# Local transformer: the norm of the MLP's rows on GpSimd behind its softmax product, its turning products and copies one step later

## The chip, the cores and the metric

One core of a Trainium2 chip runs the whole kernel, one launch. The metric is the device time of that core in microseconds, the median of several runs; lower is better.

## The reference

The kernel computes a chain of four transformer-like layers on x of shape (4, 512, 128). The change is in the third, a local transformer of six layers, 16 heads of 64, windows of 32 rows:

```
for i in range(DEPTH):                       # DEPTH = 6
    x = attn_layer(shift_tokens(x), Wqkv[i], q_scale[i], k_scale[i], Wo[i]) + x
    x = ffn_layer(shift_tokens(x), ln_g[i], ln_b[i], W1[i], b1[i], W2[i], b2[i]) + x

def ffn_layer(x, g, bln, W1, b1, W2, b2):
    mu = x.mean(-1, keepdims=True)
    var = ((x - mu) ** 2).mean(-1, keepdims=True)
    xn = (x - mu) / jnp.sqrt(var + 1e-05) * g + bln
    hg = xn @ W1 + b1
    a, gate = jnp.split(hg, 2, -1)
    return a * jax.nn.gelu(gate, approximate=False) @ W2 + b2
```

`attn_layer` makes q, k and v, scales q and k to unit length, turns them by rotary tables, takes a softmax over the own and the previous window, and projects back. All of it is float32.

## The kernel before

The four batches go through the transformer in pairs, so its six layers are twelve half-layers (`hl`, 0 to 11). The attention of a half-layer is eight steps (`w`, 0 to 7; `g` = 8 hl + w counts all 96 of them), one for every half of a unit of 128 rows by two batches. The work of several steps is in flight at once: while step g takes its softmax, the rotary products of step g + 3 and the transposes of step g + 2 are made. The order of each engine's instructions is written out by hand, in one loop over g for each engine (`tensor`, `vector`, `scalar`, `gpsimd`); engines wait for each other by counting semaphores (`s.at(name, n)`).

The MLP of a half-layer needs all rows of its attention. It is laid beside the attention of the next half-layer, in pieces. Tables `BESIDE_PE`, `BESIDE_DVE`, `BESIDE_ACT` and `BESIDE_POOL` say at which step and slot of an engine's loop a piece stands: a slot (w, n) is the n-th place in step w. Only the last half-layer's MLP stands alone, behind the loop. The pieces that matter here, in order:

- `shift`: two products (L2130, L2131) and a copy on ScalarE (L2616) put shifted rows into `XN` (8 tiles of 128x128).
- `stats` on VectorE, in step 1: mean and variance of the eight tiles (L2382, L2385, L2387).
- `guess` on ScalarE (L2585, L2587) starts the inverse root. VectorE refines it by four small products (L2307, L2310, L2313, L2316); they are handed out one by one between its other instructions (`fill`). The same four lines refine the roots that scale q and k.
- `norm` on VectorE (L2403), in step 1: eight instructions, `(XN - mean) * root`, in place.
- `turn` on TensorE (L2140): eight transposes into PSUM banks 1 and 4, and on ScalarE (L2625) two copies of them, with the norm's gain and bias, into `xT`.
- `gates`, `up`, `down`: gate products (L2152), from step 2 on, the gelus (L2635), up products (L2161), down products (L2175).

Around them, in each step: TensorE makes rotary products (L2013), value products (L2022), transposes of q and k (L2034), masks (L2050), scores (L2057), transposes of the softmax (L2072), the weighing of values (L2095), and every second step the output projection (L2116). VectorE does the rotary products (L2285, L2290), row sums of squares (L2297) and their clamp (L2301), the q scaling (L2332, it waits for the four rotary sums of its rows), the scores' maximum and difference (L2342, L2347), the row sums of the softmax (L2356) and their inverse (L2359), and a copy (L2367). ScalarE does squares (L2548), the exponential (L2592), copies (L2558, L2569, L2599, L2608). GpSimd does rotary sums (L2730), the k scaling (L2737), the softmax product (L2743) and key padding (L2753). The softmax transposes (L2072) of a step wait for its softmax product. The first gate product reads `xT` as the first copy of the turned rows leaves it, and writes bank 4, which the second copy frees.

## Time and profile before

| | us |
|---|---|
| median of 3 runs | 2585.14 |
| lowest, highest | 2583.83, 2594.27 |
| span of the profiled execution, first to last instruction | 2576.0 |
| start of half-layer 1 (its first softmax product) | 760.8 |
| start of half-layer 11 | 2129.5 |

The profiled execution has only its span; a run's time also holds what lies before the first and behind the last instruction. The transformer fills some 1,670 us of the span; a half-layer beside which an MLP runs takes 136 to 138 us.

### The profile page before, as it was taken

Reading aid. Unit: us, or ns where it says so; the run is one execution under the profiler, and the core shown is the slowest. Engines: PE = TensorE matmul, PEld = TensorE weight load, DVE = VectorE, ACT = ScalarE, POOL = GpSimd, SP = SyncE. Lnnn points to the kernel's source line nnn. Section 1 sums busy time; section 2 is a strip of 40 time slices with the busy share of each in tenths; the row PEclk is TensorE's granted clock in tenths of the full one; section 3 lists DMA queues with packets and bytes.
Section 4 is the critical chain, followed back from the end, with each engine's and each line's share of the span. In section 5 each row is a group of like instructions: output and inputs, shape, how many; then the busy total and the mean of one; then the engine's idle time right before and its main releaser. Section 6 shows DMA issues by size and latency. Waiting matters only on the chain.

```text
span 2576.0 us, 83743 instructions
## 1 busy us (share of the span) xinstructions
PE 2259.8 (88%) x36496; PEld 1557.8 (60%) x36496; DVE 1921.9 (75%) x4241; ACT 1237.9 (48%) x2267; POOL 1161.5 (45%) x854
## 2 busy tenths in 40 slices
PE   6959768975999999999999999999999999878675
PEld 3537634443666766666766666766766666645464
DVE  4553366667998888988898989898988989555612
ACT  2423233333556555565565565656565565334231
POOL 1025410004665655665565656665666556310064
PEclk9969978887999999999999999999999999889787
DMA  7101100001111111112111211121111011220012
GB/s 245 66 18 35 50 23 1 1 1 28 36 32 35 36 50 41 31 35 65 43 31 33 67 27 31 35 65 35 40 35 31 23 40 31 52 84 6 13 35 75
DMA packets 62105, 107.09 MB, mean 42 GB/s; under 512 B 11604, under 2 KB 46687, under 8 KB 55212
## 3 DMA queue, kind: packets, MB, share of 16 engines
q1 hardware_dynamic: 57004, 93.45, 12.9%
q0 software_dynamic: 4736, 8.29, 1.5%
q8 instruction: 289, 4.73, 0.8%
q14 instruction: 76, 0.62, 0.1%
HBM read 42.70 MB, written 13.24 MB: 22 GB/s over the span
## 4 chain that ended last, share of the span: by engine, by line
PE 64%; DVE 15%; issue 9%; POOL 9%; ACT 2%; DMA 1%; SPq 1%; POOLq 0%; DVEq 0%; ACTq 0%
PE ps L2013 9%; PE ps L2116 5%; PE ps L2095 5%; PE ps L2034 4%; POOL mem L2730 4%; PE ps L2022 4%; PE ps L2057 4%; PE ps L2072 3%; PE ps L2175 3%; PE ps L2161 2%; PE ps L2152 2%; PE ps L1039 2%; POOL mem L2743 2%; PE ps L559 2%; PE ps L1519 2%
## 5 line engine op out<-in xcount | busy, mean ns | idle before, releaser
L2730 POOL TENSOR_TENSOR mem<-mem 128x512 f32<-128x512 f32 x384 | 572.7, 1499 | 582.2 <-DVE mem L2290 579.0
L2013 PE MATMUL ps<-mem 128*128 128x512 f32 x768 | 383.4, 612 | 4.3 <-DVE mem L2290 2.0
L2569 ACT ACTIVATE mem<-ps 128x512 f32<-128x512 f32 x384 | 222.1, 604 | 158.0 <-PE ps L2034 157.4
L2548 ACT ACTIVATE mem<-ps 128x512 f32<-128x512 f32 x384 | 220.6, 598 | 126.9 <-PE ps L2013 86.8
L2285 DVE TENSOR_TENSOR mem<-ps,mem 128x512 f32<-128x512 f32 x384 | 258.7, 674 | 22.8 <-ACT mem L2548 22.4
L2290 DVE TENSOR_TENSOR mem<-ps,mem 128x512 f32<-128x512 f32 x384 | 261.1, 680 | 0.0
L2034 PEld LDWEIGHTS ps<-mem 128*128 128x128 f32 x1536 | 187.7, 145 | 109.7 <-issue 95.8
L2095 PEld LDWEIGHTS ps<-mem 64*64 64x64 f32 x12288 | 195.3, 137 | 83.8 <-issue 83.5
L2297 DVE TENSOR_REDUCE mem<-mem 128x16 f32<-128x1024 f32 x192 | 231.9, 1208 | 0.0
L2743 POOL TENSOR_TENSOR mem<-mem 128x1024 f32<-128x1024 f32 x96 | 182.3, 1899 | 96.2 <-DVE mem L2359 96.2
L2095 PE MATMUL ps<-mem 64*64 64x32 f32 x12288 | 208.0, 222 | 12.8 <-issue 10.5
L2034 PE MATMUL ps<-mem 128*128 128x128 f32 x1536 | 215.2, 277 | 2.3 <-POOL mem L2737 1.9
L2022 PE MATMUL ps<-mem 128*128 128x512 f32 x384 | 206.0, 619 | 10.4 <-ACT mem L2558 6.9
L2013 PEld LDWEIGHTS ps<-mem 128*128 128x128 f32 x768 | 132.5, 192 | 110.3 <-issue 90.7
L2737 POOL TENSOR_TENSOR mem<-mem 128x1024 f32<-128x1024 f32 x96 | 182.0, 1896 | 13.2 <-DVE mem L2332 13.2
L2116 PE MATMUL ps<-mem 128*128 128x128 f32 x1536 | 183.0, 279 | 2.5 <-ACT mem L2608 2.5
L2116 PEld LDWEIGHTS ps<-mem 128*128 128x128 f32 x1536 | 179.6, 195 | 8.4 <-issue 5.7
L2342 DVE TENSOR_REDUCE mem<-ps 128x8 f32<-128x512 f32 x192 | 131.2, 683 | 62.0 <-PE ps L2057 61.9
L711 ACT ACTIVATE mem<-ps,mem 77x512 f32<-77x512 f32 x192 | 115.5, 678 | 110.5 <-PE ps L541 110.5
L673 DVE TENSOR_REDUCE mem<-ps 128x8 f32<-128x616 f32 x96 | 76.3, 795 | 118.7 <-PE ps L510 118.7
L2057 PEld LDWEIGHTS ps<-mem 64*32 64x32 f32 x12288 | 128.8, 105 | 53.6 <-issue 53.6
L2057 PE MATMUL ps<-mem 64*32 64x64 f32 x12288 | 146.4, 226 | 10.8 <-issue 10.8
(294 smaller groups left out, 4173.0 us busy)
## 6 DMA issues: line engine op xcount, KB each, us to landing
mem<-mem SPq DMA_DIRECT2D x48, 768.0 KB, 5.8
mem<-in_Wqkv SPq DMA_DIRECT2D x6, 1536.0 KB, 6.8
mem<-mem SPq DMA_DIRECT2D x36, 256.0 KB, 3.5
y<-mem SPq DMA_DIRECT2D x8, 512.0 KB, 6.4
mem<-in_W12T SPq DMA_DIRECT2D x8, 512.0 KB, 7.7
mem<-y SPq DMA_DIRECT2D x16, 256.0 KB, 4.7
mem<-in_L3W SPq DMA_DIRECT2D x16, 256.0 KB, 5.8
mem<-in_L2Wo SPq DMA_DIRECT2D x6, 512.0 KB, 7.0
```

The source lines that it names most:

```text
L2013: e.matmul(self.K.ps[:, o, :], self.columns(u, bb), self.K.l2[l % 2]["Wqkv"][:, 512 * i:512 * i + 512], start=True, stop=True, skip_group_ ...
L2022: e.matmul(self.K.ps[:, k, :], self.columns(u, bb), self.K.l2[l % 2]["Wqkv"][:, 2048 + 512 * j:2560 + 512 * j], start=True, stop=True, ski ...
L2034: last = e.transpose(ps[:, o, 128 * c:128 * c + 128], self.T1[r % 2][k][:, h:h + 128], self.K.ident)
L2057: last = e.matmul(ps[row:row + 32, banks[odd], at:at + 64], self.qT[ur][64 * hp:64 * hp + 64, bb, c, 32 * wn:32 * wn + 32], self.kT[ur][64 ...
L2095: last = e.matmul(ps[64 * hp:64 * hp + 64, banks[wi], at:at + 32], src[keys, bb, 128 * c + 64 * hp:128 * c + 64 * hp + 64], self.PT[keys, ...
L2116: last = e.matmul(ps[:, k, 128 * bb:128 * bb + 128], self.oT[:, c, bb, :], self.K.l2[l % 2]["Wo"][:, c, :], start=c == 0, stop=c == 7, ski ...
L2285: e.tensor_tensor(h3(t1)[:, hh], src, bc(self.CT[:, t4, k, :], 1, 8), ALU.mult)
L2290: e.tensor_tensor(view(self.T2[:, 512 * j:512 * j + 512], "p (h a c) -> p h a c", h=8, a=2), swapped, bc(view(self.SN[:, t4, k, :], "p (a ...
L2297: e.tensor_reduce(self.ss[bb][:, H * k:H * k + H], h3(self.SQ), AX.X, ALU.add).then_inc(s("square_sums"), 1)
L2569: e.activation(to, view(self.K.ps[:, self.FEATURE[i], :], "p (c q) -> p c q", c=4), ACT.Copy).then_inc(s("placed"), 1)
L2730: e.tensor_tensor(t1[:, cols], t1[:, cols], self.T2[:, cols], ALU.add).then_inc(s("rotated"), 1)
L2743: e.tensor_tensor(p, p, bc(self.sms[g % 2], 2, 64), ALU.mult).then_inc(self.s("soft"), 1)
```

## The change

The norm of the rows moves for eleven of the twelve MLPs from VectorE's step 1 to GpSimd's step 1, behind the softmax product. VectorE signals the end of the root's refinement by a new semaphore (`mlp_rooted`), for which the norm waits. The turning products move from slots 4 and 5 of step 1 to a new slot 5 of step 2, behind the last two rotary products of that step, and their two copies from slots 2 and 3 of step 1 on ScalarE to slot 1 of step 2, behind the exponential. The last half-layer's norm stays on VectorE. The number of instructions is the same but for the refinement's semaphores.

```diff
-    BESIDE_PE = {(1, 1): (("shift", 0),), (1, 4): (("turn", 0),), (1, 5): (("turn", 1),), (2, 2): (("gates", 0),),
+    BESIDE_PE = {(1, 1): (("shift", 0),), (2, 5): (("turn", 0), ("turn", 1)), (2, 2): (("gates", 0),),
...
-    BESIDE_DVE = {(1, 0): (("stats", 0),), (1, 1): (("norm", 0),), (3, 0): (("gate", 0),), (4, 0): (("down", 0),),
+    BESIDE_DVE = {(1, 0): (("stats", 0),), (3, 0): (("gate", 0),), (4, 0): (("down", 0),),
...
-    BESIDE_ACT = {(1, 0): (("shift", 0),), (1, 1): (("guess", 0),), (1, 2): (("turn", 0),), (1, 3): (("turn", 1),),
+    BESIDE_ACT = {(1, 0): (("shift", 0),), (1, 1): (("guess", 0),), (2, 1): (("turn", 0), ("turn", 1)),
...
-    BESIDE_POOL = {(0, 0): (("kept", 0),), (4, 1): (("tables", 0),)}
+    BESIDE_POOL = {(0, 0): (("kept", 0),), (1, 0): (("norm", 0),), (4, 1): (("tables", 0),)}
...
                  if turned:
                     self.pe_rotate(e, g + 3, 2)
                     self.pe_rotate(e, g + 3, 3)
+                if this:
+                    self.pe_beside(e, hl, w, 5)
                 if placed:
                     self.pe_by_feature(e, g + 2, 0)
...
     def v_mlp_root(self, e, f, c):
         K = self.K
         e.wait_ge(*self.s.at("mlp_guessed", f + 1))
-        for _ in self.refine_root(e, K.rs[:, c], K.va[:, c], K.rt[:, c]):
-            self.mlp_root = K.v.n
-            yield
-
-    def v_norm(self, e, f):
+        yield from self.refine_root(e, K.rs[:, c], K.va[:, c], K.rt[:, c], self.s("mlp_rooted"))
+
+    def norm_rows(self, e, f):
         K, s, bp = self.K, self.s, f % 2
-        self.fill(999)
-        e.wait_ge(K.v.sem, self.mlp_root)
+        e.wait_ge(*s.at("mlp_rooted", f + 1))
         for i in range(8):
             j = 8 * bp + i
             e.tensor_scalar(K.XN[:, i, :], K.XN[:, i, :], K.mv[:, j, 0:1], K.rs[:, j:j + 1], ALU.subtract,
...
                  if this:
                     self.p_soft(e, g)
+                    self.p_beside(e, hl, w, 0)
                 if turned:
                     self.p_rotate(e, g + 3, 2)
                     self.p_rotate(e, g + 3, 3)
```

The order of instructions shows what moved, for half-layer 1 (a line of the kernel after is 1 to 5 higher than the same line before). VectorE before, in step 1, from the third small product of the root to the next rotary product:

```order
L2297 TENSOR_REDUCE mem<-mem 128x16
L2313 SCALAR_TENSOR_TENSOR mem<-mem 128x8
L2316 SCALAR_TENSOR_TENSOR mem<-mem 128x8
L2403 TENSOR_SCALAR mem<-mem 128x128 x8
L2356 TENSOR_REDUCE mem<-mem 128x16
L2359 RECIPROCAL mem<-mem 128x16
L2285 TENSOR_TENSOR mem<-ps,mem 128x512
```

VectorE after, the same place:

```order
L2298 TENSOR_REDUCE mem<-mem 128x16
L2314 SCALAR_TENSOR_TENSOR mem<-mem 128x8
L2361 TENSOR_REDUCE mem<-mem 128x16
L2317 SCALAR_TENSOR_TENSOR mem<-mem 128x8
L2364 RECIPROCAL mem<-mem 128x16
L2286 TENSOR_TENSOR mem<-ps,mem 128x512
```

The norm is gone, and the root's last small product stands behind the row sums of the softmax. GpSimd after, from the softmax product of step 1 to the q and k work of step 2 (before, the row of L2405 is not there, and the rest is the same):

```order
L2748 TENSOR_TENSOR mem<-mem 128x1024
L2405 TENSOR_SCALAR mem<-mem 128x128 x8
L2735 TENSOR_TENSOR mem<-mem 128x512 x2
L2758 COPY mem<-mem 128x16x32
L2735 TENSOR_TENSOR mem<-mem 128x512
L2742 TENSOR_TENSOR mem<-mem 128x1024
```

The norm stands ahead of two rotary sums and the padding. TensorE before, from the first turning product in step 1 to the first gate products of step 2:

```order
L2140 MATMUL ps<-mem 128x128 x4
L2022 MATMUL ps<-mem 128x512
L2140 MATMUL ps<-mem 128x128 x4
L2034 MATMUL ps<-mem 128x128 x8
L2072 MATMUL ps<-mem 128x128 x8
L2050 MATMUL ps<-mem 128x512 x2
L2057 MATMUL ps<-mem 32x64 x64
L2013 MATMUL ps<-mem 128x512 x2
L2095 MATMUL ps<-mem 64x32 x64
L2013 MATMUL ps<-mem 128x512 x2
L2034 MATMUL ps<-mem 128x128 x8
L2152 MATMUL ps<-mem 128x512 x2
```

TensorE after, the same stretch:

```order
L2024 MATMUL ps<-mem 128x512
L2036 MATMUL ps<-mem 128x128 x8
L2074 MATMUL ps<-mem 128x128 x8
L2052 MATMUL ps<-mem 128x512 x2
L2059 MATMUL ps<-mem 32x64 x64
L2015 MATMUL ps<-mem 128x512 x2
L2097 MATMUL ps<-mem 64x32 x64
L2015 MATMUL ps<-mem 128x512 x2
L2142 MATMUL ps<-mem 128x128 x8
L2036 MATMUL ps<-mem 128x128 x8
L2154 MATMUL ps<-mem 128x512 x2
```

The eight turning products stand behind the last rotary products of step 2, eight transposes ahead of the gate products.

## Rows read from the trace of the kernel before

**Rows 1.** The page, busy time of each engine and its share.
```profile
PE 2259.8 (88%) x36496; PEld 1557.8 (60%) x36496; DVE 1921.9 (75%) x4241; ACT 1237.9 (48%) x2267; POOL 1161.5 (45%) x854
```
**Rows 2.** Windows, steps 0 and 1 of half-layers 1 to 11, two of eleven.
```profile
core 0: us, PE busy (x) PEld busy (x) DVE busy (x) ACT busy (x) POOL busy (x), PEclk, DMA share, GB/s
760.80:795.82 35.02, 31.00 (x624) 20.81 (x624) 33.30 (x77) 19.23 (x38) 20.47 (x16) 1.00 0.10 26
...
1036.15:1071.17 35.02, 32.52 (x618) 21.05 (x617) 34.22 (x77) 19.11 (x37) 20.41 (x15) 0.95 0.13 33
...
sum 383.70, PE 345.16 PEld 226.38 DVE 371.67 ACT 210.58 POOL 224.72; mean PE 31.38 PEld 20.58 DVE 33.79 ACT 19.14 POOL 20.43
```
**Rows 3.** Waits: who waited for whom, us in total, times, longest.
```profile
PE ps L2140 <- DVE mem L2403: 27.1, 12, 6.3
```
**Rows 4.** Windows, step 2 of half-layers 1 to 11, their sum.
```profile
sum 226.60, PE 225.97 PEld 153.51 DVE 170.24 ACT 145.95 POOL 106.99; mean PE 20.54 PEld 13.96 DVE 15.48 ACT 13.27 POOL 9.73
```
**Rows 5.** Timeline, half-layer 1, VectorE: start, us, what, idle before it.
```profile
777.32 0.25 DVE L2313 SCALAR_TENSOR_TENSOR mem<-mem 128x8 f32<-128x8 f32 x1
...
777.81 2.14 DVE L2403 TENSOR_SCALAR mem<-mem 128x128 f32<-128x128 f32 x8
779.87 1.21 DVE L2356 TENSOR_REDUCE mem<-mem 128x16 f32<-128x1024 f32 x1
...
786.96 0.17 DVE L2307 TENSOR_TENSOR mem<-mem 128x32 f32<-128x32 f32 x1
...
790.40 1.22 DVE L2332 TENSOR_TENSOR mem<-mem 128x1024 f32<-128x1024 f32 x1
```
**Rows 6.** Timeline, half-layer 1, TensorE.
```profile
776.33 1.02 PE L2013 MATMUL ps<-mem 128*128 128x512 f32 x2
778.98 0.66 PE L2140 MATMUL ps<-mem 128*128 128x128 f32 x4 [1.62 <-DVE mem L2403]
...
783.40 1.09 PE L2072 MATMUL ps<-mem 128*128 128x128 f32 x8 [1.59 <-POOL mem L2743]
784.33 0.59 PE L2050 MATMUL ps<-mem 128*128 128x512 bf16 x2
...
793.26 1.04 PE L2034 MATMUL ps<-mem 128*128 128x128 f32 x8
794.14 2.74 PE L2152 MATMUL ps<-mem 128*128 128x512 f32 x6
```
**Rows 7.** Timeline, half-layer 1, ScalarE.
```profile
779.76 0.78 ACT L2625 ACTIVATE mem<-ps,mem 128x512 f32<-128x512 f32 x1 [0.68 <-PE ps L2140]
...
792.04 1.05 ACT L2592 ACTIVATE mem<-mem 128x1024 f32<-128x1024 f32 x1
```
**Rows 8.** Timeline, half-layer 1, GpSimd.
```profile
781.44 1.90 POOL L2743 TENSOR_TENSOR mem<-mem 128x1024 f32<-128x1024 f32 x1 [3.89 <-DVE mem L2359]
783.30 2.51 POOL L2730 TENSOR_TENSOR mem<-mem 128x512 f32<-128x512 f32 x2
...
790.57 2.19 POOL L2730 TENSOR_TENSOR mem<-mem 128x512 f32<-128x512 f32 x1 [4.20 <-DVE mem L2290]
```
**Rows 9.** Groups of GpSimd's instructions: busy us, mean ns | idle before them.
```profile
L2723 POOL TENSOR_TENSOR mem<-mem 128x128 f32<-128x128 f32 x24 | 10.5, 457 | 0.0
...
L2760 POOL COPY mem<-mem 128x512 f32<-128x512 f32 x12 | 7.4, 615 | 12.8 <-DVE mem L2374 12.8
```
**Rows 10.** Timeline, half-layer 3, TensorE before the turning products.
```profile
1054.00 0.66 PE L2140 MATMUL ps<-mem 128*128 128x128 f32 x4 [2.35 <-DVE mem L2403]
```
**Rows 11.** Windows, just behind it; columns as in rows 2.
```profile
1054.70:1058.10 3.40, 3.40 (x13) 2.37 (x12) 3.37 (x8) 1.56 (x3) 1.63 (x1) 0.50 0.00 0
```
**Rows 12.** Timeline, half-layer 0, TensorE at a granted clock of 0.50.
```profile
641.96 1.97 PE L2034 MATMUL ps<-mem 128*128 128x128 f32 x8 [1.90 <-POOL mem L2737]
643.72 1.06 PE L2050 MATMUL ps<-mem 128*128 128x512 bf16 x2
```

More of the change, by code:

```diff
@@ L1794 @@
                  (5, 4): (("down", 1),), (6, 0): (("turn_x", 1),)}
-    BESIDE_DVE = {(1, 0): (("stats", 0),), (1, 1): (("norm", 0),), (3, 0): (("gate", 0),), (4, 0): (("down", 0),),
+    BESIDE_DVE = {(1, 0): (("stats", 0),), (3, 0): (("gate", 0),), (4, 0): (("down", 0),),
                   (5, 0): (("gate", 1),), (5, 2): (("down", 1),)}
-    BESIDE_ACT = {(1, 0): (("shift", 0),), (1, 1): (("guess", 0),), (1, 2): (("turn", 0),), (1, 3): (("turn", 1),),
+    BESIDE_ACT = {(1, 0): (("shift", 0),), (1, 1): (("guess", 0),), (2, 1): (("turn", 0), ("turn", 1)),
                   (2, 2): (("gelu", 0),), (4, 1): (("turn_x", 0),), (4, 3): (("gelu", 1),), (6, 0): (("turn_x", 1),)}
-    BESIDE_POOL = {(0, 0): (("kept", 0),), (4, 1): (("tables", 0),)}
+    BESIDE_POOL = {(0, 0): (("kept", 0),), (1, 0): (("norm", 0),), (4, 1): (("tables", 0),)}
     TOTALS = dict(cleared=4, kept=16, x_normed=NT, x_turned=2 * NF, x_cols=4 * NF, tables=6 * DEPTH, qk=4 * NG, squared=4 * NG,
-                  clamped=NG, guessed=NG, mlp_variance=NF, mlp_guessed=NF,
+                  clamped=NG, guessed=NG, mlp_variance=NF, mlp_guessed=NF, mlp_rooted=NF,
                   rotated_half=4 * NG, rotated=4 * NG, square_sums=2 * NG, q_unit=NG, k_unit=NG, by_feature=4 * NG,
@@ L2186, in vector @@
         self.extra = iter(())
-        self.mlp_root = self.unit_root = 0
+        self.unit_root = 0
         for r in range(2):
@@ L2245, in vector @@
         self.v_stats(e, f)
-        self.v_norm(e, f)
+        self.fill(999)
+        self.norm_rows(e, f)
         self.next.v_start(e)
@@ L2265, in v_beside @@
                 self.v_stats(e, f)
-            elif what == "norm":
-                self.v_norm(e, f)
             elif what == "gate":
@@ L2302, in v_rotate, with refine_root @@
             self.extra = chain(self.extra, self.v_root(e, r))
-    def refine_root(self, e, y, a, tmp):
+    def refine_root(self, e, y, a, tmp, event=None):
         v = self.K.v
@@ L2315, in refine_root @@
         e.wait_ge(v.sem, t)
-        v(e.scalar_tensor_tensor(y, tmp, 5.0, y, ALU.add, ALU.mult))
+        last = e.scalar_tensor_tensor(y, tmp, 5.0, y, ALU.add, ALU.mult)
+        if event:
+            last.then_inc(event, 1)
+        else:
+            v(last)
         yield
@@ L2710, in p_beside @@
                 self.p_kept(e, f)
+            elif what == "norm":
+                self.norm_rows(e, f)
             elif what == "tables":
```

## The prediction

> **What bounds the kernel now.** I read the page first: TensorE is busy 88% of the span, VectorE 75%, GpSimd 45% [rows 1], so a gain has to come from a place where TensorE waits. Next I cut the transformer into stretches. The starts of the softmax product (L2743, one a step) mark the steps. From that of step 0 to that of step 2 of half-layers 1 to 11, TensorE is busy 345.2 of 383.7 us: it stands still 38.5 us, 3.5 us a half-layer, while VectorE is busy 371.7 us [rows 2]. In the step that follows, TensorE is busy 226.0 of 226.6 us [rows 4]: there TensorE alone sets the time, and VectorE has 5 us to spare. So this is VectorE's stage (steps 0 and 1) followed by TensorE's stage (step 2).
>
> Where TensorE waits is in the list of waits and in the timeline of half-layer 1. It waits for the norm's rows (L2403) before the turning products (L2140): 27.1 us in twelve times, of which the last, behind the last half-layer, is 6.3 [rows 3], so 1.9 us on average for eleven. Then it waits again, 1.59 us, for the softmax product before L2072 [rows 6]. Both waits hang on one chain on VectorE, which has no gap: small product 777.32, norm 777.81, row sums 779.87 [rows 5], softmax product on GpSimd 781.44 [rows 8], L2072 at 783.40 [rows 6].
>
> **The change, part by part.** I work it out for half-layer 1 and multiply by 11. All times are those of its timeline.
>
> *Norm off VectorE.* The row sums (L2356) now follow the small product that ends at 777.32 + 0.25 = 777.57, instead of starting at 779.87 [rows 5]. That is 2.30 us; the last small product now stands behind the row sums and gives back some 0.05. I take 2.25 us earlier for the row sums, the softmax product and L2072. Bounds: 2.06 (the norm's own start to the row sums' start) and 2.55 (from 777.32). TensorE's own work doesn't hold L2072: from 776.33 it has a pair of products, another such pair and eight transposes (1.02 + 1.02 + 1.04 us [rows 6]) and is done by 779.4, while L2072 is released at 783.40 - 2.25 = 781.15. So the two waits become one of about 2 us.
>
> *Turning products.* In step 1 they cost nothing, since TensorE waited there. In step 2 nothing hides them: eight transposes are 794.14 - 793.26 = 0.88 us [rows 6], all on the path.
>
> *Their copies on ScalarE.* The first gate product (L2152) reads what the first copy writes and uses the PSUM bank of the second, so it waits for both. The turning products start at 793.26 - 2.25 = 791.01. A copy started 779.76 - 778.98 = 0.78 after its turning product did [rows 6, 7]; two copies of 0.78 end at 793.35, and with 0.1 to hand over TensorE goes on at 793.4 or 793.5. Without that wait it would be there at 791.01 + 0.88 + 0.88 = 792.77. The wait is 0.68 us; bounds 0 and 1.0. ScalarE is free in time: the exponential ahead of the copies ends at 792.04 + 1.05 - 2.25 = 790.84 [rows 7]. The copies push back a feature copy, two squares and the gelus by 1.56 us; the next product that needs a gelu's bank is an up product behind the whole output projection, which covers it.
>
> *Norm on GpSimd.* No such operation is in the trace there. The nearest rows are a product of two inputs and the same width, 0.457 us, and a one-input copy of four times the width, 0.615 us [rows 9]. I take 0.457, by width and kind nearest, so 8 x 0.457 = 3.7 us; bounds 0.15 (a quarter of the copy) and 0.615 each, 1.2 to 4.9 us. Queued behind it on GpSimd are two rotary sums (2.51 us) [rows 8], then the key padding, and VectorE's q scaling (L2332) waits for the sums. The sums now end at 781.09 + 3.7 + 2.51 = 787.3; L2332 wants them at 790.40 - 2.25 = 788.15 [rows 5]. TensorE wants L2332's result only at 791.9, so it may start as late as 790.5: the norm is free up to 6.9 us, 0.86 each. Turning needs the rows at 791.0, 6 us after they are done.
>
> *The shared port.* GpSimd now works until about 788, where before it stood still for 4.20 us [rows 8]. In that pause VectorE ran its four small products of the root (the first at 786.96 [rows 5]), and each would wait for a GpSimd instruction that is under way: when VectorE ran L2332 at 790.40, the rotary sum beside it took 2.19 us, against 2.51 / 2 = 1.26 [rows 5, 8]. Each waits at most one sum, and all at most until GpSimd runs dry at 788, so VectorE may lose some 2 us, of the 2.35 that L2332 has. I book 0; little is left. The Trainium skill has this as a rule (SBUF — State Buffer, "Who interferes with whom"): a VectorE instruction with two SBUF inputs and a GpSimd instruction that reads SBUF lock each other out for a whole instruction. The trace agrees with its 2.19 us. If by that rule all four products met a whole sum, 4 x 1.26 = 5.0 us, VectorE would be 2.7 us late for TensorE, and without the clock the time would be 2585.1 + (2.7 - 0.69) x 11 = 2607; that is counted in case 5.
>
> *The last half-layer* keeps its norm on VectorE with one semaphore wait in place of another: 0.
>
> Sum without the clock: -2.25 + 0.88 + 0.68 = -0.69 us a half-layer, x 11 = -7.6 us.
>
> **The clock.** In four of these eleven stretches the granted clock reads 0.95 instead of 1.00; one of them is 1036.15 [rows 2]. There the wait before turning was 2.35 us, and right behind it the clock was 0.50 (1.2 GHz) for 3.4 us [rows 10, 11]. It fell behind four of the five longest of these waits and behind none of the six short ones such as 1.62 us [rows 6]. Today this is free: what runs slowly is followed by the second wait, which only shrinks. Behind the change there is one wait of about 2 us (0.3 more on average, as the eleven waits before turning are 1.9 on average and this one 1.62), and right behind it the work that sets the time. At half clock eight transposes take 1.97 us against 1.09, the mask products 1.06 against 0.59 [rows 6, 12]: 1.35 us lost in 3.03, so up to 1.5 us for a fall of 3.4 us. Part of a fall may lie in the wait itself, so I take 1.2 (0.5 to 1.6). How many of eleven? The new waits are longer than the six behind which it held, but one of the five longest left it at full too; I take 7 (3 to 11): 8.4 us. The Trainium skill says in TensorE: Matmul & The Clock Gate, "HAM oscillation — how this bites in real kernels", that a kernel whose bursts are parted by waits pays the slow restart on every round. In this trace four rounds of eleven show it. By that rule it would be all eleven, which is case 4.
>
> Sum: 2576.0 - 7.6 + 8.4 = 2576.8 us of span. The median of the runs, 2585.1, is 9.1 us above the span of the profiled execution; I keep that, and forecast 2585 us.
>
> **Rivals.**
> 1. *The forecast*: gain and clock cancel, 2585, its own range 2578 to 2591. Chance 0.50.
> 2. *The clock holds* (it falls twice or less). For it: waits of 1.6 us leave it at full. Against it: four falls already. 2585.1 - 7.6 = 2577.5. Chance 0.17.
> 3. *The clock holds and the copies are not waited for*, say because TensorE comes to the first gate product later than I think. Against it: nothing stands between but eight transposes. 2577.5 - 0.68 x 11 = 2570. Chance 0.11.
> 4. *The clock falls in all eleven*, at 1.6 us: +17.6 - 7.6 = 2595. Chance 0.10.
> 5. *GpSimd's norm is dear*, the side of slower: at 0.86 us each the q scaling comes late for TensorE and from 0.93 each (6.9 + 0.69 over eight) the change loses. If one costs what the 128x512 sum costs, 1.26 us, 10.1 us in all, it loses 3.2 - 0.7 = 2.5 a half-layer: 2613. Against it: one input, a quarter of the width. Chance 0.08.
> 6. *The change doesn't do what it says*: another wait holds the softmax product (the squares, the exponential), so nothing is gained in step 1, and turning and copies are paid in step 2: (0.88 + 0.68) x 11 = 17, 2602. Against it: VectorE's rows have no gap from 777.3 to 783. Chance 0.04.
>
> **Numbers.** A measurement of this kernel tells 0.5% (12.9 us) from no change: the three runs span 2583.8 to 2594.3. Faster by more, under 2572.2: case 3 and a little of case 2, 0.13. Slower by more, over 2598.1: cases 5 and 6, 0.12. Within: 0.75. The range leaves out half of case 3 and cases 5 and 6: 2572 to 2596.
>
> **What would show it.** The norm's eight rows on GpSimd, near 0.46 us each and under 0.86. The softmax product 1.9 us behind the third small product (L2313), where it is 4.12 now. One wait of 2.0 to 2.8 us before the softmax transposes, and a clock of 0.5 behind it in some 7 of 11. A wait of 0.7 us before the first gate product, on ScalarE's copies. TensorE's still time over steps 0 and 1 down from 3.5 to 2.1 to 2.5 us. I am wrong if the clock stays at 1.00, if GpSimd's rows are above 0.86 us, or if VectorE's q scaling comes more than 2 us late.

## The result, and the profile after

| | before | after |
|---|---|---|
| median of 20 runs each, us | 2582.01 | 2595.77 |
| lowest, highest | 2574.58, 2594.27 | 2583.82, 2609.45 |
| span of the profiled execution | 2576.0 | 2594.0 |

The ratio is 1.0054, 95% interval 1.0043 to 1.0065: slower by 14 us, just over the 0.5% that I had named as the bound to no change. 2595.77 lies at the very end of the range, on the side of case 5.

The page of after, its line of busy times:

```profile
PE 2264.9 (87%) x36400; PEld 1562.2 (60%) x36496; DVE 1911.7 (74%) x4153; ACT 1235.8 (48%) x2267; POOL 1227.5 (47%) x942
```

VectorE gave up the norm, eleven times 2.14 us [rows 5] or 23.5, and is only 10.2 us less busy than in [rows 1]; GpSimd took it over and is 66 us busier. The windows, cut at the same softmax products as [rows 2] (steps 0 and 1 of half-layers 1 and 2, then the sum over eleven), and the sum over step 2, as [rows 4]:

```profile
760.34:796.00 35.66, 31.66 (x623) 21.37 (x624) 31.79 (x69) 19.14 (x38) 25.85 (x23) 0.96 0.13 33
899.15:935.54 36.39, 31.63 (x608) 20.67 (x609) 33.59 (x68) 17.58 (x36) 26.66 (x24) 0.91 0.28 91
...
sum 392.41, PE 347.89 PEld 229.73 DVE 360.22 ACT 203.51 POOL 289.22; mean PE 31.63 PEld 20.88 DVE 32.75 ACT 18.50 POOL 26.29
...
sum 235.65, PE 233.23 PEld 156.54 DVE 174.26 ACT 151.85 POOL 107.06; mean PE 21.20 PEld 14.23 DVE 15.84 ACT 13.80 POOL 9.73
```

Steps 0 to 2 of the eleven half-layers take 392.41 + 235.65 = 628.06 us; before, by [rows 2, 4], 383.70 + 226.60 = 610.30. The 17.8 us between them are the whole difference of the spans of these two executions (18.0); the medians lie 13.8 us apart, so some 4 us are this pair's own. TensorE is busy 581.1 us in them, before 571.1, and stands still 46.9, before 39.2. So 10 us went to slower work of TensorE and 8 us to its waits.

Which waits, the groups of TensorE's instructions in after tell (busy us, mean ns of one | idle time ahead of it, by who ended it): rotary products, transposes of q and k, softmax transposes, first gate products, turning products:

```profile
L2015 PE MATMUL ps<-mem 128*128 128x512 f32 x768 | 388.3, 619 | 10.6 <-DVE mem L2352 7.6 <-DVE mem L2291 1.2 <-issue 0.7
L2036 PE MATMUL ps<-mem 128*128 128x128 f32 x1536 | 213.2, 275 | 10.7 <-DVE mem L2337 8.8 <-POOL mem L2742 1.9
...
L2074 PE MATMUL ps<-mem 128*128 128x128 f32 x768 | 109.2, 284 | 34.1 <-POOL mem L2748 31.5 <-issue 2.5
...
L2154 PE MATMUL ps<-mem 128*128 128x512 f32 x144 | 68.8, 615 | 1.5 <-ACT mem L2627 1.5
...
L2142 PE MATMUL ps<-mem 128*128 128x128 f32 x96 | 15.7, 316 | 7.6 <-DVE mem L2405 6.3 <-DVE mem L2291 1.2
```

Before, the same five groups idled 4.3, 2.3, 23.4, 0.0 and 27.1 us. The wait before turning is gone but for the last half-layer's 6.3 (-19.5); the one before the softmax transposes grew (+10.7); and two that were hardly there cost together 14.7: the q scaling (L2337) ahead of L2036, and the scores' difference (L2352) ahead of L2015. The copies, L2627, cost 1.5. (A group counts the whole trace.)

The timeline of half-layer 1 shows how the first of them comes about. GpSimd, VectorE and TensorE, columns as in [rows 5]:

```profile
778.69 1.90 POOL L2748 TENSOR_TENSOR mem<-mem 128x1024 f32<-128x1024 f32 x1 [1.52 <-DVE mem L2364]
780.57 6.28 POOL L2405 TENSOR_SCALAR mem<-mem 128x128 f32<-128x128 f32 x8
786.81 2.51 POOL L2735 TENSOR_TENSOR mem<-mem 128x512 f32<-128x512 f32 x2
789.26 0.63 POOL L2758 COPY mem<-mem 128x512 f32<-128x512 f32 x1
789.84 1.27 POOL L2735 TENSOR_TENSOR mem<-mem 128x512 f32<-128x512 f32 x1
```
```profile
776.93 0.26 DVE L2314 SCALAR_TENSOR_TENSOR mem<-mem 128x8 f32<-128x8 f32 x1
777.11 1.21 DVE L2361 TENSOR_REDUCE mem<-mem 128x16 f32<-128x1024 f32 x1
...
789.42 2.76 DVE L2337 TENSOR_TENSOR mem<-mem 128x1024 f32<-128x1024 f32 x1 [0.61 <-POOL mem L2735]
```
```profile
780.64 1.09 PE L2074 MATMUL ps<-mem 128*128 128x128 f32 x8 [1.93 <-POOL mem L2748]
...
789.24 1.04 PE L2142 MATMUL ps<-mem 128*128 128x128 f32 x8
792.24 1.27 PE L2036 MATMUL ps<-mem 128*128 128x128 f32 x8 [1.96 <-DVE mem L2337]
```

The row sums follow the third small product at once, as forecast, and TensorE has one wait of 1.93 us before the softmax transposes. But the norm takes 6.28 us on GpSimd where I had 3.7; the rotary sums end 789.3, and the q scaling behind them took 2.76 us in place of the 1.22 of [rows 5]. It began beside the key padding (L2758) and ended 1.07 us behind the rotary sum that follows the padding (789.84 + 1.27 = 791.11).

In half-layer 2 the same work hurts in the other way (GpSimd, VectorE, TensorE):

```profile
918.98 6.27 POOL L2405 TENSOR_SCALAR mem<-mem 128x128 f32<-128x128 f32 x8
925.21 2.50 POOL L2735 TENSOR_TENSOR mem<-mem 128x512 f32<-128x512 f32 x2
927.66 0.61 POOL L2758 COPY mem<-mem 128x512 f32<-128x512 f32 x1
```
```profile
924.01 0.18 DVE L2308 TENSOR_TENSOR mem<-mem 128x32 f32<-128x32 f32 x1
...
924.86 0.68 DVE L2347 TENSOR_REDUCE mem<-ps 128x8 f32<-128x512 f32 x1
925.46 2.85 DVE L2314 SCALAR_TENSOR_TENSOR mem<-mem 128x32 f32<-128x32 f32 x1
928.24 0.68 DVE L2352 TENSOR_TENSOR mem<-ps,mem 128x512 f32<-128x512 f32 x1
```
```profile
919.05 1.77 PE L2074 MATMUL ps<-mem 128*128 128x128 f32 x8 [2.11 <-POOL mem L2748]
...
925.27 2.07 PE L2097 MATMUL ps<-mem 64*64 64x32 f32 x128
...
928.97 1.54 PE L2015 MATMUL ps<-mem 128*128 128x512 f32 x2 [1.64 <-DVE mem L2352]
```

A product of 128x32, 0.18 us elsewhere, lasts 2.85 us: it begins 0.25 us behind GpSimd's first sum and ends at 928.31, with the padding copy behind the second sum (927.66 + 0.61). Behind it stands L2352, whose result frees what the next rotary product of TensorE needs. The product of the same size that stood beside the norm itself took 0.18 us (924.01). This holds for the whole trace: the 128x32 products that lie beside the norm take 0.18 to 0.28 us, and in each of the eleven half-layers exactly one VectorE product with two SBUF inputs is stretched, the first one that begins once the sums or the padding run. In half-layers 1, 3, 7, 10 and 11 it is the q scaling (2.76 or 2.77 us), and TensorE waits 1.2 to 2.0 us for it; in 2, 4, 8 and 9 it is the third small product, ahead of L2352 (2.83 to 3.06), and TensorE waits 1.5 to 1.9; in 5 and 6 it is the fourth, behind L2352 (2.75 and 2.86), and TensorE waits only 0.62, for a rotary product (L2291). The nine long waits are 1.7 us on average.

The clock, in windows just behind either kind of wait (columns as in [rows 2]), is at 1.2 GHz:

```profile
793.00:796.40 3.40, 3.40 (x8) 1.59 (x6) 3.37 (x6) 2.37 (x4) 2.80 (x3) 0.50 0.02 5
...
919.30:922.70 3.40, 3.18 (x90) 2.50 (x91) 2.05 (x4) 0.95 (x3) 3.40 (x5) 0.50 0.01 2
```

It fell twelve times in these stretches, before four times. Six of the twelve falls stand behind the softmax wait (half-layers 2, 4, 5, 6, 8, 9) and six behind the second wait (1, 2, 4, 8, 9, 11).

### The profile page after: what moved, and what is told of

It is laid out like the page before. It is cut to its first block, busy times and chain, and to the rows that moved or that the text cites. A ratio compares the mean times of both kernels' runs of the same rounds, so it can differ in the third digit from the quotient of the medians.

```text
span 2594.0 us, 83647 instructions
## 1 busy us (share of the span) xinstructions
PE 2264.9 (87%) x36400; PEld 1562.2 (60%) x36496; DVE 1911.7 (74%) x4153; ACT 1235.8 (48%) x2267; POOL 1227.5 (47%) x942
## 4 chain that ended last, share of the span: by engine, by line
PE 58%; DVE 16%; POOL 11%; issue 10%; ACT 3%; DMA 1%; SPq 1%; POOLq 0%; DVEq 0%; ACTq 0%
PE ps L2015 8%; PE ps L2118 5%; PE ps L2097 4%; POOL mem L2735 4%; PE ps L2024 4%; PE ps L2036 4%; PE ps L2059 3%; PE ps L2177 2%; PE ps L2074 2%; POOL mem L2748 2%; PE ps L2163 2%; PE ps L2154 2%; PE ps L1039 2%; PE ps L559 2%; PE ps L537 2%
## 5 line engine op out<-in xcount | busy, mean ns | idle before, releaser
L2015 PE MATMUL ps<-mem 128*128 128x512 f32 x768 | 388.3, 619 | 10.6 <-DVE mem L2352 7.6
L2291 DVE TENSOR_TENSOR mem<-ps,mem 128x512 f32<-128x512 f32 x384 | 260.8, 679 | 4.9 <-POOL mem L2735 4.9
L2036 PEld LDWEIGHTS ps<-mem 128*128 128x128 f32 x1536 | 184.6, 143 | 120.2 <-issue 98.4
L2036 PE MATMUL ps<-mem 128*128 128x128 f32 x1536 | 213.2, 275 | 10.7 <-DVE mem L2337 8.8
L2015 PEld LDWEIGHTS ps<-mem 128*128 128x128 f32 x768 | 133.4, 193 | 118.1 <-issue 94.5
```

The lines of the kernel that those rows point to most:

```text
L2015: e.matmul(self.K.ps[:, o, :], self.columns(u, bb), self.K.l2[l % 2]["Wqkv"][:, 512 * i:512 * i + 512], start=True, stop=True, skip_group_ ...
L2036: last = e.transpose(ps[:, o, 128 * c:128 * c + 128], self.T1[r % 2][k][:, h:h + 128], self.K.ident)
L2291: e.tensor_tensor(view(self.T2[:, 512 * j:512 * j + 512], "p (h a c) -> p h a c", h=8, a=2), swapped, bc(view(self.SN[:, t4, k, :], "p (a ...
```

## The experiments

Medians of the kernel before differ between the chips that were used (2580 to 2605 us), so every time is told as a ratio to the kernel before on the same chip. "Stretches" is the sum over steps 0 to 2 of half-layers 1 to 11 in one profiled execution, "busy" TensorE's part of it; the difference of the two is its still time.

| kernel | ratio, 95% interval | stretches, us | busy, us |
|---|---|---|---|
| before | 1 | 610.3 | 571.1 |
| after | 1.0054 [1.0043, 1.0065] | 628.1 | 581.1 |
| after_again | 1.0070 [1.0045, 1.0095] | 625.4 | 581.4 |
| e1_two_products | 0.9952 [0.9933, 0.9972] | 606.1 | 575.5 |
| e2_norm_last | 0.9969 [0.9952, 0.9986] | 604.6 | 573.2 |
| e3_turn_late_only | 1.0117 [1.0094, 1.0140] | 641.0 | 583.9 |
| e5_last_two | 1.0026 [1.0011, 1.0042] | 615.3 | 574.5 |
| e4_fill_after | 0.9990 [0.9969, 1.0010] | 614.2 | 586.0 |
| e6_fill_before | 0.9982 [0.9957, 1.0006] | 606.0 | 582.6 |
| e8_two_fill | 0.9909 [0.9880, 0.9939] | 596.6 | 582.8 |
| e8_again | 0.9940 [0.9922, 0.9958] | 595.6 | 580.0 |
| e9_last_two_hold | 0.9962 [0.9940, 0.9984] | 600.6 | 569.1 |
| e10_after_hold | 1.0062 [1.0041, 1.0082] | 625.6 | 574.9 |
| e11_turn_ahead | 0.9969 [0.9944, 0.9993] | 610.5 | 586.5 |
| e12_hold_fill | 0.9939 [0.9919, 0.9959] | 595.5 | 579.5 |
| e13_late_fill | 1.0034 [1.0018, 1.0051] | 622.7 | 600.7 |

The theories: **the queue** (A), the norm is long on GpSimd, so the sums and the q scaling come late; **the port** (B), GpSimd's sums now run where VectorE has instructions that it locks out; and **the clock**.

**A shorter norm, and a norm out of the way** (e1, e2, e3, e5). e1 makes the norm in two products over all eight tiles instead of eight instructions:

```diff
-                self.norm_rows(e, f)
+                self.p_norm(e, f)
...
+    def p_norm(self, e, f):
+        K, s, c = self.K, self.s, slice(8 * (f % 2), 8 * (f % 2) + 8)
+        rows = K.XN[:, 0:8, :]
+        e.wait_ge(*s.at("mlp_rooted", f + 1))
+        e.tensor_tensor(rows, rows, bc(K.mv[:, c, 0], 2, D), ALU.subtract).then_inc(s("mlp_centred"), 1)
+        e.wait_ge(*s.at("mlp_centred", f + 1))
+        e.tensor_tensor(rows, rows, bc(K.rs[:, c], 2, D), ALU.mult).then_inc(s("mlp_rows"), 8)
```

> The changed kernel, with GpSimd's norm as two broadcast products over all eight tiles (128x1024: subtract, then multiply) instead of eight two-scalar instructions. The 128x1024 products of this kernel take 1.9 us, so 3.8 us instead of 6.3. Theory A (GpSimd's norm is too long, the rotary sums behind it come late, VectorE's q scaling waits for them): TensorE's wait of 1.2 to 2.0 us ahead of the q and k transposes in step 2 goes, only 0.7 us for ScalarE's copies stays; 11 x 1.0 = 11 us less than the changed kernel, some 2585. Rival B (the shared port: two-input products lock VectorE out for longer than the two-scalar ones): VectorE's small products of the root and the q scaling stretch, TensorE's waits in step 2 stay at 1.5 us or more, 2595. Rival C (the granted clock's falls are the loss, not the waits): the wait before the softmax transposes is untouched, 12 falls stay 12, 2590 or more.

GpSimd's rows in e1, and the turned rows' first reader on TensorE:

```profile
796.88 1.91 POOL L2412 TENSOR_TENSOR mem<-mem 128x1024 f32<-128x1024 f32 x1
...
798.93 1.90 POOL L2414 TENSOR_TENSOR mem<-mem 128x1024 f32<-128x1024 f32 x1
```
```profile
944.01 2.81 PE L2154 MATMUL ps<-mem 128*128 128x512 f32 x6 [0.40 <-ACT mem L2635]
```
```profile
L2015 PE MATMUL ps<-mem 128*128 128x512 f32 x768 | 383.3, 612 | 4.0 <-DVE mem L2291 1.4 <-DVE mem L2352 1.2 <-ACT mem L2551 0.6
L2036 PE MATMUL ps<-mem 128*128 128x128 f32 x1536 | 211.0, 274 | 2.3 <-POOL mem L2750 1.9 <-DVE mem L2337 0.4
```

3.9 us for the same norm, the 3.7 that I had forecast for the other form. Both new waits are gone (the last two rows idle as before the change), the copies cost the 0.40 us, and the kernel is 0.5% faster than before the change: the length of the norm on GpSimd decided the sign. The first wait is 1.9 to 2.1 us, and the clock falls behind it in nine of eleven.

e2 leaves the eight instructions and puts them behind the two sums and the key padding:

```diff
                 if this:
                     self.p_soft(e, g)
-                    self.p_beside(e, hl, w, 0)
                 if turned:
                     self.p_rotate(e, g + 3, 2)
                     self.p_rotate(e, g + 3, 3)
...
+                if this:
+                    self.p_beside(e, hl, w, 0)
```

> The changed kernel with GpSimd's norm (eight instructions, 6.3 us) behind the two rotary sums and the key padding instead of ahead of them. Theory A (late rotary sums): the sums end 6.3 us earlier, the q scaling never waits; but the norm now ends near 790.0 of half-layer 1, 0.8 us behind the turning products' turn, and the next rotary sum waits 2 us for it. TensorE's wait in step 2 about 0.8 to 1.2 us instead of 1.7, 5 to 10 us less: 2588. Rival B (port): VectorE's small products meet short instructions instead of back to back sums, so the 2.85 us small product is gone; the same sign, so this run tells A and B apart only by which row shrinks. Rival C (clock alone): 2590 or more.

The norm's row is even longer there, and it costs less, since no rotary sum stands behind it:

```profile
805.11 6.85 POOL L2405 TENSOR_SCALAR mem<-mem 128x128 f32<-128x128 f32 x8
```

What TensorE waits for in step 2 is 0.2 to 1.1 us, for the norm itself or the copies, and the ratio is 0.9969. VectorE's q scaling now stands beside the norm and takes 1.21 to 1.35 us there.

e3 undoes the move to GpSimd and keeps turning and copies in step 2:

```diff
-    BESIDE_DVE = {(1, 0): (("stats", 0),), (3, 0): (("gate", 0),), (4, 0): (("down", 0),),
+    BESIDE_DVE = {(1, 0): (("stats", 0),), (1, 1): (("norm", 0),), (3, 0): (("gate", 0),), (4, 0): (("down", 0),),
...
-    BESIDE_POOL = {(0, 0): (("kept", 0),), (1, 0): (("norm", 0),), (4, 1): (("tables", 0),)}
+    BESIDE_POOL = {(0, 0): (("kept", 0),), (4, 1): (("tables", 0),)}
...
+            elif what == "norm":
+                self.fill(999)
+                self.norm_rows(e, f)
```

> The changed kernel with the norm back on VectorE in step 1 as before: only the turning products and their copies stand a step later. Theory M (the move itself costs the turning products' 0.88 us, a 0.7 us wait for the copies, and a longer single wait ahead of the softmax transposes behind which the clock falls): nothing is gained on VectorE, 11 x 1.56 = 17 us and up to 11 falls of 1.2 us on top of the kernel before, 2599 to 2612, slower than the changed kernel. Rival A alone (all of the loss is GpSimd's norm and what is queued behind it): 2582, as before.

TensorE in half-layer 2 of e3, and the window just ahead and behind:

```profile
948.22 1.97 PE L2074 MATMUL ps<-mem 128*128 128x128 f32 x8 [4.49 <-POOL mem L2751]
```
```profile
947.10:950.50 3.40, 2.28 (x10) 1.86 (x10) 3.37 (x5) 0.00 (x0) 3.40 (x3) 0.50 0.00 0
```

One wait of 4.3 to 4.5 us, the clock at 1.2 GHz behind all eleven (for some 3.4 us in four of them, for some 7 us in seven), 1.0117. This half of the change alone costs over 1%.

e5 is e1 and e2 together: two products, behind the sums.

> Both edits: GpSimd's norm as two 128x1024 products, behind the rotary sums and the padding. Theory A: sums end near 783, norm near 787.5, turning at 789.2 finds its rows, the next rotary sum is not late. TensorE's step-2 wait is the copies' 0.7 us: 2583, or 2575 to 2580 if the clock falls less often too. Rival B (port): the small products of the root (784.2 to 786.3) fall into the two products of 1.9 us each and wait for them, up to 3 us late, TensorE waits 1 to 2 us for the PSUM bank of the scores: 2593. Rival C (clock): 2590 or more.

This parts the two theories. The queue is as short as it can be and no sum stands behind the norm, yet e5 loses 0.7% to e1. GpSimd and VectorE in half-layer 1, and TensorE behind them:

```profile
795.94 1.90 POOL L2412 TENSOR_TENSOR mem<-mem 128x1024 f32<-128x1024 f32 x1
...
797.98 1.90 POOL L2414 TENSOR_TENSOR mem<-mem 128x1024 f32<-128x1024 f32 x1
```
```profile
796.57 1.32 DVE L2308 TENSOR_TENSOR mem<-mem 128x32 f32<-128x32 f32 x1
...
798.41 1.51 DVE L2311 SCALAR_TENSOR_TENSOR mem<-mem 128x32 f32<-128x32 f32 x1
```
```profile
801.30 1.98 PE L2015 MATMUL ps<-mem 128*128 128x512 f32 x4 [1.45 <-DVE mem L2352]
```

The two small products here end with the GpSimd product beside them (797.9, 799.9) and take 1.3 to 1.5 us for 0.18; TensorE waits for L2352 in every half-layer, up to 1.46 us. A alone would have made e5 the fastest of the four.

**The clock by itself** (after_again, e4, e6, e8). In the wait before the softmax transposes (in e6: in the wait before the turning products) a value product that is due there anyway is made three times instead of once, each time with the same result:

```diff
+                if more and hl >= 1 and w == 1:
+                    self.pe_spare(e, u + 1, 3, 2)
...
+    def pe_spare(self, e, u, n, times):
+        (bb, j), k = divmod(n, 2), self.VALUES[n]
+        hl, l, bp, t4 = self.place(u)
+        after(e, self.freed[k])
+        for _ in range(times):
+            e.matmul(self.K.ps[:, k, :], self.columns(u, bb), self.K.l2[l % 2]["Wqkv"][:, 2048 + 512 * j:2560 + 512 * j],
+                     start=True, stop=True, skip_group_check=True)
```

> The changed kernel itself, unchanged, so that the others of this call can be read against it on the same chip. Every theory: 1.005 times the kernel before.

> The changed kernel with TensorE kept at work in the 2.1 us wait ahead of the softmax transposes: the value product that stands ahead of it is made three times into the same bank (2 x 0.86 us more), nothing else. Theory C (what the wait costs is the half clock behind it): the falls right behind this wait go, those behind the step-2 wait stay, 12 falls become some 6, 1.2 us each: 7 us less than the changed kernel, 1.002 to 1.003 times the kernel before. Rival: falls cost nothing that shows (the loss is waits alone): the same as the changed kernel, or slower by up to 4 us where the repeated products delay the softmax transposes.

> The kernel before with the same two extra value products in its wait of 1.6 to 2.3 us ahead of the turning products. The step of the prediction that a fall there is free today: the four falls go and the time stays within 2 us of the kernel before (1.000). Rival: a fall costs there too: 1.2 us x 4 to 5 = 5 us faster (0.998).

> The variant with GpSimd's norm as two products (0.995 times the kernel before, a fall of the clock behind the softmax wait in ten of eleven half-layers) plus the extra value products in that wait. Theory C: all ten falls go, 1.2 us each, 12 us less: 0.991. Rival (a fall costs nothing here): 0.995.

The change repeats its loss on another chip, 1.0070, with eleven falls. With the filling (e4) it is 0.9990 on the same chip: the clock falls twice, although a wait of 1.6 to 1.95 us stays in step 2 of ten half-layers, and the stretches shorten by 11.2 us although TensorE is busy longer. That is more than expected: falls behind the second wait went too. In the kernel before (e6) the filling also keeps the clock up, and the ratio, 0.9982, can't be told from 1, nor from the rival's 0.998. The stretches say more: the four that had a fall before (half-layers 3, 5, 6, 9) add up to 219.3 us there and to 219.8 in e6, so there the falls cost nothing that shows; the 4.3 us by which the sum of all eleven is shorter lie in the other seven. In e1 (e8) the filling takes the kernel to 0.9909. TensorE in half-layer 2 of e8:

```profile
929.42 1.99 PE L2035 MATMUL ps<-mem 128*128 128x512 f32 x4
...
933.54 1.09 PE L2084 MATMUL ps<-mem 128*128 128x128 f32 x8 [0.40 <-POOL mem L2766]
```

The extra products fill 1.7 of the 2.1 us, and no fall is left in the eleven stretches, which shorten from 606.1 to 596.6 us. e1 and e8 ran on different chips.

**What the instruction costs, and the small products held back** (e7, e9, e10, e11). e7 makes the tiles in pairs by four forms on GpSimd; six of the eight tiles are not normalised:

```diff
+            if i < 2:
+                e.tensor_scalar(x, x, mean, root, ALU.subtract, ALU.mult).then_inc(done, 1)
+            elif i < 4:
+                e.tensor_scalar(x, x, root, None, ALU.mult).then_inc(done, 1)
+            elif i < 6:
+                e.tensor_scalar(x, x, 0.5, 0.01, ALU.subtract, ALU.mult).then_inc(done, 1)
+            else:
+                e.tensor_scalar(x, x, 0.01, None, ALU.mult).then_inc(done, 1)
```

> The price of GpSimd's instruction by itself. The changed kernel, but the eight tiles of a norm are treated in four ways, two tiles each: as in the norm (two operations, two per-partition scalars), one operation with a per-partition scalar, two operations with constants, one operation with a constant; the rows are not normalised, so only the durations count. Theory 1 (the per-partition scalars are dear): 0.79, 0.6, 0.3, 0.3 us. Theory 2 (each operation of the pair is a pass over the tile): 0.79, 0.45, 0.79, 0.45. Theory 3 (a two-scalar instruction has a fixed cost of its own whatever its operands): 0.79 in all four.

Groups of GpSimd's instructions in e7: L2416 is the first form, L2418 the second, L2420 the third, L2422 the fourth:

```profile
L2416 POOL TENSOR_SCALAR mem<-mem 128x128 f32<-128x128 f32 x22 | 17.3, 792 | 0.0
...
L2420 POOL TENSOR_SCALAR mem<-mem 128x128 f32<-128x128 f32 x22 | 13.9, 642 | 0.0
...
L2418 POOL TENSOR_SCALAR mem<-mem 128x128 f32<-128x128 f32 x22 | 13.3, 612 | 0.0
...
L2422 POOL TENSOR_SCALAR mem<-mem 128x128 f32<-128x128 f32 x22 | 11.3, 527 | 0.0
```

None of the theories had this. The least form takes 0.53 us; a second operation adds 0.12, and a scalar for each partition some 0.08 each (0.792 against 0.642 for two, 0.612 against 0.527 for one). Even the least is dearer than the 0.457 of a product of two inputs [rows 9].

e9 is e5 with VectorE's four small products for q and k held back through the first slots of step 2 (they are handed out later, and no work is left out); e10 does the same to after:

```diff
+                self.hold = hl >= 1 and w == 2
...
+                self.hold = False
...
+        if self.hold:
+            return
```

> The variant with GpSimd's norm last and in two products (1.0026 times the kernel before; TensorE waited 0.2 to 1.5 us for VectorE's L2352 in all eleven half-layers), with VectorE's four small products of the q and k root held back in step 2 until the q scaling asks for them, so that none stands between the scores' instructions. Theory B (one small two-input product locked out by a 1.9 us product on GpSimd holds up the scores' PSUM bank): that wait goes, 11 x 1.0 = 11 us and the falls behind it: 0.997 or less. Rival (the scores are late for another reason, such as TensorE's own order): 1.0026.

> The changed kernel with the same hold. Theory A and B together: in the changed kernel either the small product (2.85 us, in the half-layers where TensorE waits for L2352) or the late rotary sums (1.96 us, where it waits for the q scaling) cost the same 1.7 us. Holding the small products takes away the first and leaves the second: every half-layer shows the wait for the q scaling, 1.9 to 2.3 us, and the time stays, 1.004 to 1.008 times the kernel before. Rival (the port alone makes the loss): 0.998 to 1.000.

In e9 the wait for L2352 is gone from every half-layer, in nine of them 0.2 to 0.43 us for the q scaling is left, and the ratio falls from 1.0026 to 0.9962 (on another chip; the stretches from 615.3 to 600.6 us): same queue, same norm, other neighbours. That shows that a small product held by GpSimd costs TensorE time.

In e10 the time stays at 1.0062, as expected, but not only for the expected reason. TensorE waits 1.15 to 2.89 us for the q scaling in every half-layer; VectorE and TensorE in half-layer 1:

```profile
801.82 2.43 DVE L2313 TENSOR_TENSOR mem<-mem 128x32 f32<-128x32 f32 x1
```
```profile
806.24 1.97 PE L2036 MATMUL ps<-mem 128*128 128x128 f32 x8 [2.89 <-DVE mem L2342]
```

The small products now stand right ahead of the q scaling, and the first of them is itself held for 2.25 to 2.44 us in all eleven. So e10 moves the port's cost to another place and doesn't take it away. What the long norm's queue would cost without the port no run shows. What e1 and e2 do show is that the waits of after go when the rotary sums run earlier.

e11 is e8 with turning ahead of the last two rotary products, to hide the copies:

```diff
-    BESIDE_PE = {(1, 1): (("shift", 0),), (2, 5): (("turn", 0), ("turn", 1)), (2, 2): (("gates", 0),),
+    BESIDE_PE = {(1, 1): (("shift", 0),), (2, 6): (("turn", 0), ("turn", 1)), (2, 2): (("gates", 0),),
...
+                if this:
+                    if w == 2:
+                        self.pe_beside(e, hl, w, 6)
```

> The best so far (norm as two products on GpSimd, value products repeated in the softmax wait, 0.991), with the turning products of step 2 ahead of its last two rotary products instead of behind them. The 0.4 us wait of the first gate product for ScalarE's copies is then covered: 11 x 0.4 = 4 us, 0.989. Rival: ScalarE's exponential, which stands ahead of the copies, holds them anyway: 0.991.

Both expectations fell: the turning products then wait for VectorE to release PSUM bank 1 (L2304), 14.4 us in eleven times, the clock falls in five half-layers, and e11 is slower than e8 (stretches 610.5 against 596.6 us). The group of the turning products in e11:

```profile
L2155 PE MATMUL ps<-mem 128*128 128x128 f32 x96 | 17.0, 333 | 20.7 <-DVE mem L2304 14.4 <-DVE mem L2418 6.3
```

**The best version again, and the bare move** (e13, e12, e8_again). e13 is e3 with the value product made four more times, e12 is e9 with it made twice more.

> The variant in which only the turning products move (norm on VectorE, 1.0117 times the kernel before, one wait of 4.4 us ahead of the softmax transposes and a fall of the clock behind it in eleven of eleven) with that wait filled by the value product four more times (3.4 us). Theory: without the falls only the move's own terms stay, turning products 0.88 us and copies 0.4 us, x 11 = 14 us: 1.0055. Rival (the falls cost little, the move costs 2.7 us a half-layer by waits): 1.0117.

> The variant with GpSimd's norm last, in two products, and VectorE's small products held back (0.9962), plus the value product repeated twice in the softmax wait. Its waits of step 2 are 0.2 to 0.4 us; without the falls 5 to 8 us less: 0.993 to 0.994. Rival: the filled wait gives nothing here: 0.996.

> The fastest so far once more, beside the others: 0.991 (it had 0.988 to 0.994). If it comes out at 0.995 or more, the gain ascribed to the falls was the chip's scatter.

e13 comes to 1.0034 with no fall of the clock, against 1.0117 of e3: of the 1.17% that the late turning costs on its own, 0.34 is the move (turning and copies in the stage where nothing hides them) and 0.8, some 21 us, the clock. The two ran on different chips; their stretches differ by 18.3 us. e12 and e8_again end together, 0.9939 and 0.9940: with the port's products held back or the norm ahead of them, 0.6% under the kernel before. e8 was 0.9909 in its first measurement; the intervals overlap (0.9922 to 0.9958 and 0.9880 to 0.9939), so 0.6 to 0.9% is what can be said. Either way it is faster than the kernel before and than the changed one. What the filling gave to e1 is less sure: from 0.9952 to 0.9940 or 0.9909 the intervals overlap, and it is the stretches (606.1 against 596.6 and 595.6 us) that speak for some 10 us.

## Why the prediction was wrong

The sum of the prediction beside what the traces show, for eleven half-layers:

| term | forecast, us | measured, us |
|---|---|---|
| two waits of step 1 become one, turning paid in step 2 | -15.1 | -14.5 |
| copies waited for | +7.5 | +1.5 |
| q scaling and L2352 waited for | 0 | +14.7 |
| clock | +8.4 | +16.4 |
| sum | +0.8 | +18.1 (the stretches: 17.8) |

The first measured term: of the groups above, counted inside the eleven stretches alone, the wait before turning gave back 19.5 us and the one before the softmax transposes took 11.4 (11.1 became 22.5), together -8.1. From it I take 6.4 that belong to the clock: before the change the wait of 1.59 us stands in seven of the eleven stretches alone, and in the four with a fallen clock the slow work had filled it (4 x 1.59). The clock's 16.4 are these 6.4 and the 10.0 by which TensorE is busier.

- **Norm off VectorE: right.** I had 2.25 us for the shift. On average over the eleven, the softmax product of step 1 stands 17.87 us behind that of step 0 where it was 20.25 behind it, 2.38. One wait of 1.93 to 2.11 us before the softmax transposes in all eleven, 2.0 forecast.
- **Turning: right**, eight transposes in 1.04 us (0.88 to the next instruction), now on the path.
- **Copies: right in kind, too dear.** 0.40 us in e1, e8 and e13, where nothing else is late, against 0.68. In after another wait stands ahead of them and leaves 1.5 us for all eleven.
- **Norm on GpSimd: this step failed.** "I take 0.457, by width and kind nearest", with 0.615 as the upper bound, gave 3.7 us; the eight rows take 6.28 us, 0.79 each. A product of two inputs was no measure for an instruction with two operations and two scalars for each partition, nor was a copy a bound (e7). With the norm at 3.9 us (e1) the sum comes out near the forecast: no second wait, nine falls, and stretches 4.2 us shorter than before, where I had 0.8 longer. The Trainium skill says in GPSIMD Engine Reference, "4.1 Engine selection", that with one input GpSimd is roughly at VectorE's rate; the rows here differ for this form: it took 0.34 us each on VectorE and 0.79 on GpSimd.
- **"The norm is free up to 6.9 us, 0.86 each": this failed too.** At 6.28 us it should have cost nothing. The slack of 2.35 us ran from the q scaling as it was. In half-layer 1 the sums came 1.7 us later than the q scaling wanted them (789.42, against 788.15 less the 0.46 us by which this trace's half-layer starts sooner), the scaling took 1.54 us more (2.76 for 1.22, beside a rotary sum), and TensorE needed 8.60 us from the softmax transposes to turning where it had needed 9.86, mostly since a gap of 0.79 us in its issue did not come back. That is 4.5 us against 2.35, and 1.96 us of wait. Without the 1.54 of the scaling it would have been 3.0 against 2.35, so in this half-layer, as an estimate from these numbers, the late sums alone explain some 0.6 us and the port the rest.
- **The shared port: booked at 0 while the text had it at up to 2 us. This failed as well.** One product is held in each of the eleven half-layers. This adds 24 us to VectorE: L2337 takes 124.3 us in all where it took 116.7, the third small product for q and k 28.3 where it took 17.5, the fourth 22.9 where it took 17.5. (The clamp, L2302, which now stands beside the norm and not beside the sums, got 12.5 us shorter; so VectorE's total hides half of this.) The groups of after:

```profile
L2337 DVE TENSOR_TENSOR mem<-mem 128x1024 f32<-128x1024 f32 x96 | 124.3, 1295 | 3.2 <-POOL mem L2735 3.1
...
L2314 DVE SCALAR_TENSOR_TENSOR mem<-mem 128x32 f32<-128x32 f32 x96 | 28.3, 295 | 0.1
...
L2317 DVE SCALAR_TENSOR_TENSOR mem<-mem 128x32 f32<-128x32 f32 x96 | 22.9, 238 | 0.1
```

  I had let each product wait at most one sum, by rule and row alike; a product was in fact held over two sums and the padding copy (2.85 us). That such a hold turns into waits of TensorE is shown by e5 against e9.
- **The clock: right behind the wait that I had, missing behind the one that I hadn't.** "I take 7" falls at 1.2 us behind the softmax wait; there were six (seven in after_again). The other six of the twelve stand behind the second wait, which the prediction did not have, so they belong to the failed steps above. One fall cost 16.4 / 12 = 1.4 us, inside the bounds. "Today this is free" fits e6. By the rule on oscillation that the prediction cites from the Trainium skill (TensorE: Matmul & The Clock Gate, "HAM oscillation — how this bites in real kernels"), every round pays. Waits of about 2 us did not do that: they were followed by a fall in six, seven and nine of eleven rounds (after, after_again, e1); only e3, with waits of 4.3 to 4.5 us, had it in all eleven.
- **The base.** A run of after lasts 1.9 us longer than its span (2595.93 against 2594.0). Of the 9.1 us that I kept between span and median, some 7 were therefore scatter; with 20 runs the kernel before has 2582.0 and not 2585.1.
- **The signs of being wrong were set too loose.** The clock fell, the norm's rows stayed under 0.86 us, and the q scaling of half-layer 1 began 1.7 us late, under my 2; yet the change lost. The still time over steps 0 and 1 gave it away: 4.0 us a half-layer, where I had 2.1 to 2.5.
- **The rivals.** Case 5, a dear norm, had the right mechanism on the right side, and its point of decision, 0.93 us each, was too high: 0.79 was enough together with the port. Case 4, at 17.6 us for the clock, came near its 16.4, beside costs that it didn't have. Case 6 was wrong: the softmax product did move.

Not settled: what the late sums would cost without the port; what sets from one half-layer to the next where VectorE stands when the sums begin; and why the hold lasts so long in after. In e1 the same two sums run back to back, and a small product is held by one of them alone, up to 1.03 us (GpSimd, then VectorE, in half-layer 2 of e1):

```profile
935.66 2.49 POOL L2743 TENSOR_TENSOR mem<-mem 128x512 f32<-128x512 f32 x2
```
```profile
935.94 1.03 DVE L2308 TENSOR_TENSOR mem<-mem 128x32 f32<-128x32 f32 x1
```

So e1 shortened the queue and the hold at once. How much of e8's 0.9909 to 0.9940 is chance is open too.

## What to carry to other kernels

An instruction that is moved to GpSimd should be priced by a row of its own form (operations and scalars for each partition counted). If there is no such row, use a form that has one: two broadcast products over eight tiles took 3.9 us, as the 128x1024 product of [rows 8] lets one expect, where eight instructions took 6.3, and this edit alone turned +0.5% into -0.5%. The price of GpSimd's time is not only its queue: count VectorE's instructions with two SBUF inputs that will stand beside it, each at the length of all the GpSimd instructions that run there without a gap, and take as slack only what is left behind that. When two short waits of TensorE are merged into one of 2 us ahead of the work that sets the time, count a fall of the clock in most rounds, and try to fill the wait with a product that changes nothing: it gave back 0.8% of the time in e4, and 0.1 to 0.4% where the second wait was gone already (e8).

## What the runs showed of the hardware that was not expected

- GpSimd's two-operation instruction with two scalars for each partition on 128x128 float32 takes 0.79 us; the forms with less take 0.64, 0.61 and 0.53 (e7), all more than a product of two tiles, 0.457 [rows 9].
- A VectorE product of 128x32 that takes 0.18 us alone took 2.83 to 3.06 us in after beside two rotary sums and a padding copy of GpSimd that ran one behind the other: it did not get in between them. In e1 it did: there it was held by one sum at a time (0.4 to 1.03 us). In e5, beside two products of 1.90 us with a gap of 0.14 us, it was held for one only (1.32 and 1.51 us). The Trainium skill, SBUF — State Buffer, "Who interferes with whom", has the lock for the length of an instruction; the rows of e1 and e5 agree, those of after are longer.
- Beside the eight norm instructions on GpSimd, VectorE's small products took 0.18 to 0.28 us: they were not held, though the rule that the prediction went by would have had them wait.
- The clock of TensorE stood at 1.2 GHz behind waits of 1.9 to 2.1 us in nine of eleven half-layers of e1, and at full speed in all eleven when extra products left 0.2 to 0.4 us of the wait (e8). In seven of eleven half-layers of the kernel before it stayed at full; six of these had waits of 1.5 to 1.8 us, one had a wait of 2.34.
